# Last stage of a gated two-layer transformer on one Trainium2 core: where the second expert product is scaled, and which engine prepares three small statistics

## The reference

```python
def expert(w1, bb1, gg1, bbe1, w2, bb2, gg2, bbe2):
    h = relu(_layernorm(xf @ w1 + bb1, gg1, bbe1))
    return _layernorm(h @ w2 + bb2, gg2, bbe2)
# _layernorm(x, g, b) = (x - mean) * rsqrt(var + 1e-5) * g + b
weights = softmax(top-2 of xf @ gate_W + gate_b)
out = sum over the two chosen experts of weights * expert(...) + xf
x   = x + tanh(g_ffn[1]) * out      # xf: x, layer-normed without gain
```

## Time and profile before

| what | value |
|---|---|
| median of 3 runs | 2147.1 us (2144.46 to 2152.93) |
| the profiled execution | 2151.43 us, of it 2149.6 us between its first and last instruction |
| busy over the whole span | PE 96%, DVE 81%, ACT 65%, POOL 59% |
| granted TensorE clock | 0.984 of full speed, mean |
| last stage | from about 1546 us to the end, 64 batches |

### The profile page before, as it was taken

One profiled execution on the slowest core, in us unless ns is written; L12 is line 12 of the kernel. 1 busy time (PEld: TensorE's weight loads), 2 busy tenths in 40 slices (PEclk: granted clock), 3 DMA queues, 4 the chain that ended last, 5 costly groups with the idle time before them and its releaser, 6 DMA issues.

```text
span 2149.6 us, 57692 instructions
## 1 busy us (share of the span) xinstructions
PE 2058.6 (96%) x19788; PEld 1795.7 (84%) x19788; DVE 1737.7 (81%) x4788; ACT 1394.5 (65%) x2978; POOL 1269.6 (59%) x2056
## 2 busy tenths in 40 slices
PE   6999999999699999999699999999899999999997
PEld 5888888888599999999588888888788888888885
DVE  5889888888588888888577787777588888888886
ACT  4766666666487877878366666666566666666663
POOL 5787888887300000000477878777378878878786
PEclk9999999999799999999899999999999999999998
DMA  7555221221466666666322222222100000000000
GB/s 230 187 180 166 67 65 61 69 64 53 158 239 226 247 223 246 221 244 213 133 69 71 71 75 71 75 71 66 45 23 30 29 28 29 30 30 30 30 26 18
DMA packets 151664, 226.11 MB, mean 105 GB/s; under 512 B 20454, under 2 KB 135786, under 8 KB 141036
## 3 DMA queue, kind: packets, MB, share of 16 engines
q1 hardware_dynamic: 145260, 205.99, 28.5%
q0 software_dynamic: 6144, 16.79, 2.5%
HBM read 153.77 MB, written 68.94 MB: 104 GB/s over the span
## 4 chain that ended last, share of the span: by engine, by line
PE 65%; DVE 15%; POOL 9%; issue 6%; DMA 3%; ACT 1%; POOLq 0%; SPq 0%; DVEq 0%; ACTq 0%
PE ps L1255 10%; PE ps L1271 10%; PE ps L1127 10%; PE ps L1112 6%; DVE u2g L1328 4%; PE ps L1066 4%; PE ps L1203 3%; PE ps L1215 3%; DVE h_st L1297 3%; PE ps L1159 3%; POOL k_rs L614 2%; PE ps L1083 2%; PE ps L1060 2%; PE ps L1096 2%; PE ps L1026 2%
## 5 line engine op out<-in xcount | busy, mean ns | idle before, releaser
L1397 DVE TENSOR_REDUCE nmax<-ps 128x16 f32<-128x2048 f32 x128 | 292.4, 2284 | 29.4 <-PE ps L1083 29.0
L874 ACT ACTIVATE prob_t<-ps 128x2048 f32<-128x2048 f32 x128 | 240.9, 1882 | 77.8 <-PE ps L1066 77.8
L696 POOL COPY slot_in<-slot_all 128x1 int32<-128x1 int32 x64 | 11.4, 179 | 472.9 <-DMA eo_d<-eo 472.9
L1026 PE MATMUL ps<-w2f,a_t 128*128 128x256 f32 x1024 | 233.3, 381 | 0.0
L1255 PE MATMUL ps<-xgt_hi,w_hl 128*128 128x256 f32 x1248 | 230.0, 282 | 1.0 <-DVE xgt_lo L1662 1.0
L1271 PE MATMUL ps<-w_hl,hid_hi 128*128 128x256 f32 x1248 | 226.9, 284 | 0.0
L1026 PEld LDWEIGHTS ps<-w2f,a_t 128*128 128x128 f32 x1024 | 190.9, 191 | 23.8
L670 POOL TENSOR_TENSOR km_r<-qk,cst 128x512 fp32r<-128x512 f32 x128 | 133.7, 1044 | 127.7 <-ACT qk L864 127.7
L946 ACT ACTIVATE hid<-ps,b_in 128x256 f32<-128x256 f32 x312 | 146.0, 469 | 82.6 <-PE ps L1255 67.2
L1255 PEld LDWEIGHTS ps<-xgt_hi,w_hl 128*128 128x128 f32 x1248 | 195.5, 189 | 1.4 <-issue 1.4
L1271 PEld LDWEIGHTS ps<-w_hl,hid_hi 128*128 128x128 f32 x1248 | 191.5, 188 | 0.0
(11 more groups left out here) (229 smaller groups left out, 6247.7 us busy)
## 6 DMA issues: line engine op xcount, KB each, us to landing
w_raw<-in_w_dram SPq DMA_DIRECT2D x78, 1024.0 KB, 6.8
c_t<-in_ctx_in_dram SPq DMA_DIRECT2D x128, 128.0 KB
x_d<-x SPq DMA_DIRECT2D x128, 128.0 KB
slots_d<-zeros SPq DMA_DIRECT2D x12, 1024.0 KB, 6.2
eo_d<-zeros SPq DMA_DIRECT2D x12, 1024.0 KB, 5.3
xg<-slots_d SPq DMA_DIRECT2D x39, 256.0 KB, 2.7
eo_d<-eo SPq DMA_DIRECT2D x39, 256.0 KB, 2.2
x_in<-in_x_dram SPq DMA_DIRECT2D x64, 128.0 KB
```

The lines of the kernel that those rows point to most:

```text
L874: nc.scalar.activation(prob_t[:].rearrange("p a k -> p (a k)"), scores.rearrange("p a k -> p (a k)"), ACT.Exp, scale=SOFT).then_inc(y["exp ...
L1026: mm = pe.matmul(dst, a_t[:, b.parity, e, c, :], w2f[:, e, c, :], start=False, stop=True, skip_group_check=True)
L1397: nc.vector.tensor_reduce(nmax[:, b.parity, :, 0:4], scores.rearrange("p a (r k) -> p a r k", k=P), AX_X, ALU.max, negate=True).then_inc(y ...
```

## The change

The second product leaves PSUM in two instructions of 128x512 (`out_of_psum`), multiplied by the gain alone, each right behind the statistics of its half. `u2g` gets two buffers. ScalarE then multiplies its four tiles by `k_rw` in place, behind `xft_hi` and ahead of `z`. VectorE adds eps to the variances in `h_mv`, `k_mv` and `fmv` and negates the mean in `fmv`, so that GpSimd's chains start with the power; GpSimd's first halving moves behind the power for the first product. New waits keep the single buffers of `h_mv` and `k_mv` from being overwritten early.

```diff
# GpSimd, fstep
-                        pool.wait_ge(f["u_done"].of(b - 1), f["u_done"].at(b - 1))
-                    nc.gpsimd.tensor_tensor(k_rs[:, 0, :], k_mv[:, :, 1], eps.to_broadcast([P, E1]), ALU.add)
+                        pool.wait_ge(f["u_scaled"].of(b - 1), f["u_scaled"].at(b - 1))
+                    nc.gpsimd.tensor_tensor(k_rs[:, 1, :], k_mv[:, :, 1], neg_half.to_broadcast([P, E1]), ALU.pow)
...
-                    nc.gpsimd.tensor_tensor(frs[:, 0:1], fmv[:, 1:2], eps, ALU.add)
-                    nc.gpsimd.tensor_tensor(frs[:, 1:2], frs[:, 0:1], neg_half, ALU.pow)
-                    nc.gpsimd.tensor_tensor(frs[:, 2:3], fmv[:, 0:1], frs[:, 1:2], ALU.mult)
-                    nc.gpsimd.tensor_tensor(frs[:, 3:4], frs[:, 2:3], neg_one, ALU.mult)
+                    nc.gpsimd.tensor_tensor(frs[:, 1:2], fmv[:, 1:2], neg_half, ALU.pow)
+                    nc.gpsimd.tensor_tensor(frs[:, 3:4], fmv[:, 0:1], frs[:, 1:2], ALU.mult)
# ScalarE, fstep, between xft_hi and z
+                b = s - 2
+                    act.wait_ge(f["u_done"].of(b), f["u_done"].at(b))
+                    act.wait_ge(f["k_rstd"].of(b), f["k_rstd"].at(b))
+                    for e in range(E1):
+                        nc.scalar.activation(u2g[:, b.parity, e, :], u2g[:, b.parity, e, :], ACT.Copy, scale=k_rw[:, e:e + 1])
# VectorE
+                dve.wait_ge(sig.of(b), sig.at(b, 2 * E1))          # in stats_in_all
+                nc.vector.tensor_scalar(mv[:, :, 1], mv[:, :, 1], eps, None, ALU.add)
+            def out_of_psum(b, half):
+                if (b - 2).begun:
+                    dve.wait_ge(f["halved"].of(b - 2), f["halved"].at(b - 2))
+                nc.vector.tensor_tensor(u2g[:, b.parity, two, :], ps[:, 6 + half, :], g2_in[:, two, :], ALU.mult)
-                    dve.wait_ge(f["k_rstd"].of(b), f["k_rstd"].at(b))          # fstep, b = s - 2
-                    for e in range(E1):
-                        nc.vector.scalar_tensor_tensor(out=u2g[:, e, :], in0=ps[...], scalar=k_rw[:, e:e + 1], in1=g2_in[:, e, :],
-                                                       op0=ALU.mult, op1=ALU.mult)
+                    out_of_psum(b, 0)          # b = s - 1, behind stats(..., 0)
+                    nc.vector.tensor_scalar(fmv[:, 1:2], fmv[:, 1:2], eps, None, ALU.add)
+                    nc.vector.tensor_scalar(fmv[:, 0:1], fmv[:, 0:1], -1.0, None, ALU.mult)
+                    out_of_psum(b, 1)          # b = s - 1, behind stats(..., 1)
+                        dve.wait_ge(f["k_rstd"].of(b - 1), f["k_rstd"].at(b - 1, 1))
```

More of the change, by code:

```diff
@@ L314, in flamingo_gated @@
         k_rw = psb("k_rw", [P, E1])
-        u2g = psb("u2g", [P, E1, D])
+        u2g = psb("u2g", [P, 2, E1, D])
         u2s = psb("u2s", [P, 2, D])
@@ L623, in fstep @@
                         pool.wait_ge(f["xf_done"].of(b - 1), f["xf_done"].at(b - 1))
-                    nc.gpsimd.tensor_tensor(frs[:, 0:1], fmv[:, 1:2], eps, ALU.add).then_inc(st.sem, 1)
+                    nc.gpsimd.tensor_tensor(frs[:, 1:2], fmv[:, 1:2], neg_half, ALU.pow).then_inc(st.sem, 1)
                     pool.wait_ge(st.of(b), st.at(b, 1))
[L626 to L630, removed]
+                    nc.gpsimd.tensor_tensor(frs[:, 3:4], fmv[:, 0:1], frs[:, 1:2], ALU.mult).then_inc(st.sem, 1)
                 b = s - 1
@@ L779, in fstep @@
                         .then_inc(f["x_hi_done"].sem, 1)
+                b = s - 2
+                if b.within(B):
+                    act.wait_ge(f["u_done"].of(b), f["u_done"].at(b))
+                    act.wait_ge(f["k_rstd"].of(b), f["k_rstd"].at(b))
+                    for e in range(E1):
+                        nc.scalar.activation(u2g[:, b.parity, e, :], u2g[:, b.parity, e, :], ACT.Copy, scale=k_rw[:, e:e + 1])\
+                            .then_inc(f["u_scaled"].sem, 1)
                 b = s
@@ L1304, in stats_in_all @@
                     nc.vector.bn_aggr(mv[:, e, :], st[:, e, :]).then_inc(sig.sem, 1)
+                dve.wait_ge(sig.of(b), sig.at(b, 2 * E1))
+                nc.vector.tensor_scalar(mv[:, :, 1], mv[:, :, 1], eps, None, ALU.add).then_inc(sig.sem, 1)
+            def out_of_psum(b, half):
+                if (b - 2).begun:
+                    dve.wait_ge(f["halved"].of(b - 2), f["halved"].at(b - 2))
+                two = slice(2 * half, 2 * half + 2)
+                nc.vector.tensor_tensor(u2g[:, b.parity, two, :].rearrange("p e n -> p (e n)"), ps[:, 6 + half, :],
+                                        g2_in[:, two, :].rearrange("p e n -> p (e n)"), ALU.mult).then_inc(f["u_done"].sem, 1)
             def fstep(s):
@@ L1380, in fstep @@
                     nc.vector.bn_aggr(fmv[:], fst[:]).then_inc(f["st"].sem, 1)
+                    dve.wait_ge(f["st"].of(b), f["st"].at(b, 2))
+                    nc.vector.tensor_scalar(fmv[:, 1:2], fmv[:, 1:2], eps, None, ALU.add).then_inc(f["st"].sem, 1)
+                    nc.vector.tensor_scalar(fmv[:, 0:1], fmv[:, 0:1], -1.0, None, ALU.mult).then_inc(f["st"].sem, 1)
                 b = s - 1
```

41 lines of the change are left out of this document (16 added, 25 removed).

## The result

The changed kernel takes 2150.6 us (median of 20 runs, 2148.8 to 2154.3) against 2146.6 (2143.0 to 2152.9): a ratio of 1.002, with an interval of 1.0013 to 1.0027. It is slower by 4 us, inside the range that was forecast (2137 to 2159) and on the other side of "1 us faster". The profiled execution has a span of 2148.7 us.

A forecast was written before the change was run, and what follows sets the result against it. The prediction took a VectorE–GpSimd ring of 9.02 us a step as the bound, replaced by another of 9.02; ends +0.6 us, low terms -5, high +6, less 1 us for rounding: 2146 us from 2147.1, range 2137 to 2159.

The forecast's parts named there:

- 1 us faster: Whole kernel, main case: 2146 us against 2147.1, with 1 us taken off for small terms rounded up; chance 0.70.
- the ring u2g, `k_mv`, `k_rw`: Last stage, kernel before: VectorE from `u2g` to `k_mv`, then GpSimd to `k_rw` and back, sets the step at 9.02 us.
- TensorE's 8.79: Last stage: TensorE's step without its 0.23 us wait for `z`; as the bound, 2135 us, chance 0.12.
- the first ring: Changed last stage: new ring from `xf`'s turning through TensorE, VectorE, GpSimd and ScalarE to `xf`, 9.02 us a step.
- TensorE's wait for `z`: Last stage: 0.23 us a step in the kernel before, claimed to go with the change.
- The lock: Small VectorE operations held during a large GpSimd one; priced at 0 to 0.1 us for `k_mv`'s eps.
- that rival: Small operations on `fmv` held by GpSimd: step 9.38 us, 22 us more, 2169 us; chance of port holds 0.11.
- The scalings: ScalarE's four scalings: 0.508 us for one, 0.40 each with overlap, 1.71 in all; chance of being late 0.07.
- The ceiling: Last stage: the most any gain could reach, 60 x 0.23 = 14 us, 0.6% of the kernel.
- The wait for `xf`: Changed last stage: TensorE's turning would wait 0.1 to 0.3 us a step for `xf`, in place of `z`.
- the ends of the stage: Behind the last batch: chain longer by a PSUM read and eps, shorter by GpSimd's addition, +0.6 us once.
- the second ring: Changed last stage: new ring through ScalarE's scalings, GpSimd's additions and powers, `xf` and its turning, 8.84 us a step.

The follow-up runs named there:

- Number 9: Changed kernel with GpSimd's wait for `gwt_done` moved from between the power for `k_rs` and `k_rw` to ahead of that power: 2147.75 us, 0.9992.
- number 2: Changed kernel with VectorE's second read of PSUM moved behind `k_mv` and its eps: 2147.7 us, 0.9999.
- number 5: Changed kernel with `frs` ahead of `k_rs` and `k_rw` on GpSimd and the second PSUM read behind `k_mv` and its eps: 2126.5 us, 0.9919.
- number 7: Changed kernel with the second PSUM read behind `k_mv`'s eps, and that eps split into four operations of 128x1: 2148.3 us, 1.0009.
- number 4: Kernel before with only the eps and sign operations moved from GpSimd to VectorE: 2191.2 us, 1.0206.
- number 8: Changed kernel with `u2s` ahead of the power for h on GpSimd, as in the kernel before: 2315.3 us in one run.
- number 3: Changed kernel without the eps move: scalings on ScalarE, but GpSimd still adds eps and negates the mean: 2185.3 us, 1.0188.

## Why the prediction was right and where it failed

**Right.** The bound (the ring u2g, `k_mv`, `k_rw`), and TensorE's 8.79 as the next one (8.80 measured in three kernels). The ring that took the place of the old one, in all its links. That TensorE's wait for `z` would go and one for `xf` come. The lock: the operations of 128x1 on `fmv` (60 of each between 1550 and 2100 us) took 214 and 143 ns on average inside `u2t`, never held, and that rival fell; the one of 128x4 comes too late in the changed kernel to be held for long. The scalings: 0.50 us one and 0.40 from start to start.

**Right in kind, off in size.** The ceiling was put at 14 us; the best that any kernel here gave is 2126.5 us, 17 us below before by the ratio and 19 by the medians; the steps account for 60 x (9.077 - 8.80) = 17 us. The wait for `xf` was to be 0.1 to 0.3 us a step; the row has 0.60 for the loads, and the step less TensorE's 8.80 is 9.16 - 8.80 = 0.36. The step was to stay between 8.95 and 9.1; it is 9.18 on average.

DVE's groups of the changed kernel, 1550 to 2100 us (busy us, mean ns | idle before):

```profile
L1305 DVE TENSOR_SCALAR k_mv<-k_mv,cst 128x4 f32<-128x4 f32 x59 | 13.5, 229 | 2.1
L1385 DVE TENSOR_SCALAR fmv<-fmv,cst 128x1 f32<-128x1 f32 x60 | 12.8, 214 | 2.1
```

The Trainium skill (SBUF — State Buffer, "Who interferes with whom") says that `tensor_scalar` can enter a two-port mode, and so contend with GpSimd, when its operands meet conditions that stand elsewhere. The trace agrees as far as it goes: the same operation on the same engine was held at 128x4 and not held at 128x1, so the operation's name alone doesn't tell.

**Wrong: the step in which I took 1 us off.** The forecast had 9.02 against 9.02, "since most of my small terms were rounded up, I take 1 us less". They weren't. Term by term:

| term of the first ring | forecast | measured |
|---|---|---|
| TensorE, turning to half of the second product | 2.10 | 2.16 |
| VectorE, pick-up to `k_mv`'s eps | 4.07 | 4.06 |
| GpSimd, pick-up to the end of `frs` | 2.16 | 2.24 |
| ScalarE and pick-ups | 0.69 | 0.69 |

The forecast was short of GpSimd's term by 0.08: 0.06 of it is a wait instruction that its sequencer runs between the power and `k_rw` (L614 in the chain above), and 0.02 lies between `k_rw` and `frs`. Number 9 took the 0.06 out, and the step fell by 0.07. It was short of TensorE's term by 0.06: the two turning matmuls take 0.44 us as a pair where they took 0.38.

Both sizes stand in the trace of the kernel before, in steps that I hadn't read. In all 24 steps outside the loop the power and `k_rw` look like this, 1.16 us from start to start, where all 40 inside it have 1.09 to 1.10:

```profile
1618.64 1.01 POOL L614 TENSOR_TENSOR k_rs<-k_rs,cst 128x4 f32<-128x4 f32 x1
1619.80 0.20 POOL L617 TENSOR_TENSOR k_rw<-k_rs,gw 128x4 f32<-128x4 f32 x1
```

In the changed kernel it is 1.16 outside the loop too, and in 25 of the 40 steps inside. And 10 of the 64 turnings of the kernel before took 0.43 to 0.44 us. This is one:

```profile
1857.91 0.20 PEld L1017 LDWEIGHTS ps<-cst,xf 128*128 128x128 f32 x2 [0.25 <-ACT xf L773]
1857.91 0.44 PE L1017 MATMUL ps<-cst,xf 128*128 128x128 f32 x2
```

`xf` came 0.05 us ahead of this turning, and the first load of weights starts with the first matmul; in the step of the earlier trace rows `xf` came 0.23 ahead and the load started 0.18 ahead. Over the twelve kernels of this document all 326 pairs of 0.43 us and more have their first load at most 0.011 us ahead of the matmul, and all 437 of at most 0.39 have it 0.06 or more ahead. It isn't the idle time that costs: six of the ten slow pairs of the kernel before start at the usual distance (0.23 us) from the matmul ahead of them. So a ring that closes through `xf` pays 0.06 us by the very fact that `xf` comes last, and the forecast took the pair from a step in which it didn't. VectorE's longest term, 13 pieces, was right to 0.01.

**Wrong: the ends of the stage.** Forecast +0.6 us, measured -3.2. I counted what the last batch's chain gains and loses in operations and not that the old ring held TensorE back once more there: 2.5 us of waiting and 1.7 us of slower matmuls behind it.

**Wrong: the second ring,** 8.84 against 9.16 in a loop step of number 2, which is that ring. Of the 0.32 us the hold and the pick-up behind it are 0.14 (from the start of the addition to the power 0.84, forecast 0.70), the start of `u2s` 0.08, the wait instruction 0.06 and the pair of turnings 0.06; the other terms give 0.02 back. The hold was priced for the first ring; in the second it stands between two of GpSimd's own instructions. That brought this ring level with the first in the loop.

Put right, the sum is 60 x 0.10 - 3.2 = +3 us. The sign of a difference of 4 us in 2150 hung on 0.14 us out of 9.02. I took the bound's length from one step, and the two sizes that make up the 0.14 stood in others of the same trace. With one step read, the rows allowed to keep both ends of that sum and to leave the guess at its sign out.

## What to carry to other kernels

Cutting a ring pays only down to the next one, and the next one may be made by the order in which one engine serves two readers: here GpSimd computed `k_rw`, which could wait by then (the scalings had 1.3 us of room in the run with `frs` first), ahead of `frs`, on which `xf` and TensorE hung. After a dependency is removed, ask for each queue that served it whether its order still fits; one swapped pair of blocks was worth more than the whole change (23 us against -4). And a half of a change that costs 2% by itself is not thereby a bad half. Where a forecast hangs on a tenth of a microsecond a step, take each term from many steps, inside a hardware loop and outside of it, and from steps in which the instruction is late as well as from those in which it is early.

## What the runs showed of the hardware

- GpSimd's additions of 128x256 held a VectorE tensor_scalar of 128x4 (all in SBUF) until 0.03 us behind their own end, up to 0.63 us in place of 0.23, and never one of 128x1 (120 on `fmv` and 243 on `k_mv`, all started inside such an addition, 0.22 us at most). A power of 128x1 on GpSimd didn't hold it: in number 5 the tensor_scalar of 128x4 started 14 times inside one and took 0.24 us at most.
- A second wait, long met, cost 0.065 us where GpSimd's sequencer ran it between two dependent instructions (0.143 us from end to start in place of 0.078), and nothing that shows ahead of the first (number 9).
- Small operations of VectorE that read and write 128x1 started 0.12 us apart in a row (number 7); a dependent one of 128x4 behind its wait cost 0.25 in all (number 4).
- Two turning matmuls took 0.44 us as a pair where their weights came at the last moment, and 0.38 where the first load could start 0.06 us or more ahead.
- TensorE's granted clock fell after it had idled 1.8 to 2.5 us: to 0.86 over a step of 12.6 us (number 8, in about every second step, though all had the same 1.8 us in one piece) and to 0.66 over 5 us behind the waits of 2.20 and 0.29 us in the kernel before. In number 3, with up to 1.3 us idle in one piece, and in the changed kernel, with up to 0.6 in the steps from 1600 to 2090 us, it stayed at 1.00.
